# Attention: the first group's q and k buffers are filled and loaded during the norms' stage, and a third pair of score banks serves the second pass where it runs alone

## The reference

```python
x = x + _layernorm(_L0_attn_ref(_layernorm(x), ...))   # state-space block: project, scan, out_proj
h = layernorm(_layernorm(x), ln1_g, ln1_b)             # "norms' stage": this, qkv and rope
q, k, v = split(h @ Wqkv)
q, k = (rope(q), rope(k))
scores = jnp.einsum('bqhd,bkhd->bhqk', q, k) / math.sqrt(hd)
scores = jnp.where(causal, scores, -1e9)
probs = jax.nn.softmax(scores, axis=-1)
attn = jnp.einsum('bhqk,bkhd->bqhd', probs, v) @ Wproj
...                                                    # residual, norm, top-2 of 8 experts, final norm
```

## Time and profile before

| what | us |
|---|---|
| median of 3 runs | 4084.34 (4078.41 to 4086.13) |
| profiled execution: its own time | 4088.92 |
| profiled execution: span | 4087.3 |
| PE busy in the span | 3407.1 (83%) |
| DVE / ACT / POOL busy | 2777.7 / 2461.5 / 1913.2 |
| attention stage, first instruction to its last store | 2157.4 to 3394.5 |

### The profile page before, as it was taken

The page is one execution under the profiler, slowest core; times in us unless marked ns, Lnnn a source line. Parts: engine busy times, 40 slices in busy tenths (PEclk is TensorE's granted clock), DMA queues, the critical chain, the costliest instruction groups (busy, mean ns, idle before and its releaser), DMA issues. The chain is left out here.

```text
span 4087.3 us, 69747 instructions
## 1 busy us (share of the span) xinstructions
PE 3407.1 (83%) x22940; PEld 2105.2 (52%) x22940; DVE 2777.7 (68%) x4397; ACT 2461.5 (60%) x3860; POOL 1913.2 (47%) x1734
## 2 busy tenths in 40 slices
PE   7568888888888888885876999999999996499994
PEld 3246666666666666664553333333333334366663
DVE  3259999999899999995764777777777753511113
ACT  3259999999999999993220555555555563122111
POOL 1049999999899999995431000000010002512222
PEclk9779999999999999998995999999999997599997
DMA  5633333333333333335634011011011014333323
GB/s 187 187 89 97 97 99 97 95 94 96 93 96 101 96 94 94 94 94 203 221 119 124 9 20 17 9 20 20 7 20 20 7 48 132 129 81 84 86 53 93
DMA packets 162170, 349.72 MB, mean 86 GB/s; under 512 B 20963, under 2 KB 74198, under 8 KB 147344
## 3 DMA queue, kind: packets, MB, share of 16 engines
q1 hardware_dynamic: 129904, 270.96, 23.9%
q0 software_dynamic: 20624, 43.82, 4.2%
q10 hardware_dynamic: 11280, 30.41, 2.0%
HBM read 245.04 MB, written 102.59 MB: 85 GB/s over the span
## 5 line engine op out<-in xcount | busy, mean ns | idle before, releaser
L516 POOL TENSOR_TENSOR scan_hC<-scan_hh,scan_cbc 128x512 f32<-128x512 f32 x1024 | 1376.4, 1374 | 84.5 <-DVE scan_hh L728 76.8
L728 DVE TENSOR_TENSOR_SCAN scan_hh<-scan_dA,scan_state,scan_bx 128x512 f32<-128x512 f32 x1024 | 1243.5, 1263 | 140.9 <-PE scan_bx L820 63.7
L1572 PE MATMUL attend_s<-attend_kt,attend_qt 32*128 32x512 f32 (+3 forms) x2560 | 803.3, 616 | 34.4 <-DMA attend_qt<-attend_zero 27.8
L820 PE MATMUL scan_bx<-kept_ident,scan_dBxT 128*128 128x128 f32 x4096 | 668.9, 289 | 151.0 <-DVE scan_hh L728 121.9
L564 ACT ACTIVATE scan_dA<-scan_dt,scan_an 128x512 f32<-128x512 f32 x1028 | 661.4, 712 | 30.5 <-DVE scan_hh L728 30.5
L820 PEld LDWEIGHTS scan_bx<-kept_ident,scan_dBxT 128*128 128x128 f32 x4096 | 487.7, 147 | 358.8 <-DVE scan_hh L728 243.2
L831 PE MATMUL scan_acc<-kept_ident,scan_hC 128*128 128x128 f32 x4128 | 646.4, 283 | 29.6 <-POOL scan_hC L516 22.6
L1593 PE MATMUL attend_s<-attend_qt,attend_kt 32*128 32x512 f32 (+3 forms) x2560 | 643.6, 588 | 16.3 <-POOL attend_pb L1449 13.9
L569 ACT ACTIVATE scan_dBxT<-scan_dtxT,scan_bt 128x512 f32<-128x512 f32 x1028 | 655.4, 711 | 0.2
L1483 DVE TENSOR_REDUCE attend_mx<-attend_s 128x1 f32<-128x512 f32 x768 | 494.9, 686 | 203.1 <-PE attend_s L1572 202.0
L1543 ACT ACTIVATE attend_pb<-attend_s 128x1024 f32<-128x1024 f32 x384 | 390.8, 1024 | 285.9 <-PE attend_s L1593 285.9
(11 more groups left out here) (208 smaller groups left out, 3838.1 us busy)
## 6 DMA issues: line engine op xcount, KB each, us to landing
scan_xs<-scratch_xin SPq DMA_DIRECT2D x288, 256.0 KB, 6.2
scan_cbc<-scratch_crows SPq DMA_DIRECT2D x64, 1024.0 KB, 4.8
scratch_y<-scan_uu ACTq DMA_DIRECT2D x17, 1024.0 KB, 5.7
scratch_exp_in<-proj_cleared SPq DMA_DIRECT2D x8, 1044.0 KB, 8.4
experts_xt<-scratch_exp_in SPq DMA_DIRECT2D x8, 1044.0 KB, 5.2
scratch_xin<-proj_out_x SPq DMA_DIRECT2D x8, 1024.0 KB, 5.9
scratch_sz<-proj_out_z SPq DMA_DIRECT2D x8, 1024.0 KB, 6.3
mix_yf<-scratch_y SPq DMA_DIRECT2D x8, 1024.0 KB, 6.6
```

Of the source, the lines that this page charges most:

```text
L516: pool.tensor_tensor(hC[n % 2][:, m, :], h[:, m, :], rows, ALU.mult).then_inc(hc_ok, 1)
L728: dve.tensor_tensor_scan(hh[n % 2][:, m, r], dA[n % 2][:, m, r], bx[bank(l, j)][:, r], state[:, d, n, m:m + 1], ALU.mult, ALU.add).then_in ...
L820: last = pe.transpose(bx[bank(l, j)][:, t * P:(t + 1) * P], dBxT[turned_slot(l, n)][:, t, m * P:(m + 1) * P], k["ident"][:, :])
L1572: pe.matmul(s1[v % S1][:, 0:w], qt[n % SETS][rows, t * P:(t + 1) * P], kt_[n % SETS][rows, c * C:c * C + w], start=True, stop=True).then_i ...
```

## The change

It has two parts.

1. Buffers `qt` and `kt` of set 0 and their semaphore `loaded` move out of `attend` into a stage `heads` that is opened before `mix_and_qkv` and closed at the end of the program. POOL fills them as its first work in `mix_and_qkv`. After its last load there, SP waits for the fills and for the stores of four chunks, and issues group 0's q and k (8 transfers). The zero row is no longer loaded for groups 0 and 1, since q's fill is zero. In `attend` only set 1 is filled, SP starts with v, and PE waits for 8 transfers.
2. The three banks of the first pass become one tensor `s1_all`. From step 302 on (`ALONE`), when the first pass has used them last, the pairs of the second pass go round three buffers (`s1_all[:, 0:2]`, `s2_0`, `s2_1`); a pair then waits for the exponential three pairs back instead of two.

```diff
+def first_heads(s):
+    return {
+        "qt": s.sb("qt", [P, L]),
+        "kt": s.sb("kt", [P, L]),
+        "filled": s.sems("filled")[0],
+        "loaded": s.sems("loaded")[0],
+    }
+
+def load_heads(sp, qk, qt, kt, n, loaded):
+    HG = 4
+    b, g = n // (H // HG), n % (H // HG)
+    for h in range(HG):
+        rows = slice((g * HG + h) * HD, (g * HG + h + 1) * HD)
+        own = slice(32 * h, 32 * h + HD)
+        sp.dma_start(qt[own, :], qk[b, 0, rows, :]).then_inc(loaded, 16)
+        sp.dma_start(kt[own, :], qk[b, 1, rows, :]).then_inc(loaded, 16)
...
@@ mix_and_qkv, SP after its loads, and POOL at its start
+            sp.wait_ge(heads["filled"], 2)
+            for it in range(ITEMS):
+                sp.wait_ge(stored_h[it], 16 * NC)
+            load_heads(sp, qk, heads["qt"], heads["kt"], 0, heads["loaded"])
 
         @block.gpsimd
         def _(pool):
+            pool.memset(heads["kt"][:, :], 1.0).then_inc(heads["filled"], 1)
+            pool.memset(heads["qt"][:, :], 0.0).then_inc(heads["filled"], 1)
             for i in range(2):
                 pool.memset(vt[i][:, :, :, HD:], 1.0).then_inc(ones_ok, 1)
@@ attend
-        qt = [s.sb(f"qt{i}", [P, L]) for i in range(SETS)]
-        kt_ = [s.sb(f"kt{i}", [P, L]) for i in range(SETS)]
+        qt = [heads["qt"], s.sb("qt1", [P, L])]
+        kt_ = [heads["kt"], s.sb("kt1", [P, L])]
...
-        s1 = [s.ps(f"s1_{i}", [P, C]) for i in range(S1)]
+        s1_all = s.ps("s1", [P, S1, C])
+        s1 = [s1_all[:, i, :] for i in range(S1)]
...
+        ALONE = NUNIT - LEAD + 2
+
+        def pair_bank(at, pair):
+            if at < ALONE:
+                return s2[pair]
+            third = (at - ALONE) * 2 + pair
+            return s1_all[:, 0:2, :] if third % 3 == 0 else s2[third % 3 - 1]
...
-            load(0)
             for b in range(B):
                 sp.dma_start(vall[:, b * KT:(b + 1) * KT, :, :].rearrange("p t h e -> p t (h e)"),
                              vav[:, b * KT:(b + 1) * KT, :]).then_inc(loaded_v[b], 16)
...
-            for i in range(SETS):
-                pool.memset(kt_[i][:, :], 1.0).then_inc(filled, 1)
-                pool.memset(qt[i][:, :], 0.0).then_inc(filled, 1)
+            pool.memset(kt_[1][:, :], 1.0).then_inc(filled, 1)
+            pool.memset(qt[1][:, :], 0.0).then_inc(filled, 1)
             pool.memset(zero[:, :], 0.0).then_inc(filled, 1)
             pool.memset(cap_s[:, :], 3.0e38).then_inc(filled, 1)
...
-                    own, score = pb[at % PB][:, 2 * pair:2 * pair + 2, :], s2[pair]
+                    own, score = pb[at % PB][:, 2 * pair:2 * pair + 2, :], pair_bank(at, pair)
...
-                    pe.wait_ge(loaded[n % SETS], (n // SETS + 1) * HG * 3 * 16)
+                    pe.wait_ge(loaded[n % SETS], (n // SETS * 3 + 2) * HG * 16)
...
-                if at:
+                if at >= ALONE:
+                    pe.wait_ge(exp_ok, at * 2 - 2 + pair)
+                    if at == ALONE and pair == 0:
+                        pe.wait_ge(s1_read, NUNIT * HG)
+                        pe.wait_ge(m_rows, GROUPS * NC)
+                elif at:
                     pe.wait_ge(exp_ok, at * 2 - 1 + pair)
```

More of the change, by code:

```diff
@@ L1330, in qkv_layout, with attend @@
     return np.ascontiguousarray(np.concatenate([qk, w[:, :, 2].reshape(D, D)], 1))
-def attend(nc, k, qk, va, attn, load_next):
+def attend(nc, k, heads, qk, va, attn, load_next):
     KT = L // P
@@ L1374, in attend @@
         sums = [s.sb(f"sums{i}", [P, C]) for i in range(2)]
-        s1 = [s.ps(f"s1_{i}", [P, C]) for i in range(S1)]
+        s1_all = s.ps("s1", [P, S1, C])
+        s1 = [s1_all[:, i, :] for i in range(S1)]
         s2 = [s.ps(f"s2_{i}", [P, 2, C]) for i in range(2)]
         pv = s.ps("pv", [P, C])
-        pm = s1[0][0:HG * JT, 0:P]
-        loaded = s.sems(*[f"loaded{i}" for i in range(SETS)])
+        pm = s1_all[0:HG * JT, 0, 0:P]
+        ALONE = NUNIT - LEAD + 2
[4 more added lines that the diff above has]
+            return s1_all[:, 0:2, :] if third % 3 == 0 else s2[third % 3 - 1]
+        loaded = [heads["loaded"], s.sems("loaded1")[0]]
         loaded_v = s.sems(*[f"loaded_v{b}" for b in range(B)])
@@ L1393, in _ @@
         def _(sp):
-            sp.wait_ge(filled, 2 * SETS + 1)
+            sp.wait_ge(filled, 3)
             def load(n):
@@ L1398, in load @@
                     sp.wait_ge(s2_mm, (n - SETS + 1) * NSTEP * 2)
[L1399 removed]
+                load_heads(sp, qk, qt[n % SETS], kt_[n % SETS], n, loaded[n % SETS])
+                if n < SETS:
+                    return
                 for h in range(HG):
[L1401 to L1403 removed]
                     sp.dma_start(qt[n % SETS][32 * h + HD:32 * h + HD + 1, :], zero[h:h + 1, :]
@@ L1592, in scores2 @@
                     rows = slice(32 * h, 32 * h + 32)
-                    last = pe.matmul(s2[pair][:, i, o:], kt_[n % SETS][rows, kt * P:(kt + 1) * P],
+                    last = pe.matmul(pair_bank(at, pair)[:, i, o:], kt_[n % SETS][rows, kt * P:(kt + 1) * P],
                                      qt[n % SETS][rows, qc * C + o:(qc + 1) * C], start=True, stop=True)
@@ L2304, in sandwich_block, with load_next @@
                       a["dskip"])
[L2305 to L2322, removed]
-                    combine(nc, k, x3, x1t, out)
+        with Stage(nc, "heads") as around_heads:
+            heads = first_heads(around_heads)
+            mix_and_qkv(nc, k, heads, y, sz, a["u"], a["out_wT"], a["g1"], a["b1ln"], a["wqkv"], a["rope"], x1, xf, qk, va)
+            with Stage(nc, "routed") as early:
+                rt = route_inputs(nc, early)
+                def load_next(sp):
+                    load_route_weights(sp, rt, a["wproj"], a["g2"], a["b2ln"], a["wgate"], a["expert_iota"])
+                    for n in range(2):
+                        load_route_chunk(sp, rt["at"][n], rt["xt"][n], rt["loaded"][n], n, attn, xf)
+                attend(nc, k, heads, qk, va, attn, load_next)
+                with Stage(nc, "weights") as held:
+                    ew = expert_weights(nc, held)
+                    route(nc, k, rt, attn, xf, x3[0:NTOK, :], exp_in, a["token"],
+                          lambda sp, e: load_expert_weights(sp, ew, e, a["w1"], a["b1"], a["w2"], a["b2"]))
+                    with Stage(nc, "last") as last:
+                        x1t = [last.sb(f"x1t{n}", [P, JT, D]) for n in range(B * NC)]
+                        run_experts(nc, k, ew, exp_in, a["w1"], a["b1"], a["w2"], a["b2"], x3, x1, x1t,
+                                    last.sems("loaded_x1")[0])
+                        combine(nc, k, x3, x1t, out)
```

4 lines of the change are left out of this document (2 added, 2 removed).

## The result

| | us | runs |
|---|---|---|
| before | 4084.20 median (4078.41 to 4086.13) | 4 |
| after | 4061.34 median (4058.54 to 4066.37) | 4 |
| ratio | 0.9948, 95% interval 0.9930 to 0.9965 | |

The account below looks back on a forecast made before the run. No engine bounds the whole program, its stages following each other through barriers. Handover 14.3 plus second pass 4.5 less closing block 0.6 made 18.2 us off 4084.34, so 4066.1 us; 8-in-10 range 4057 to 4075.

Parts of the forecast that it names:

- the 14.3 us: Handover to the attention: PE's first matmul comes 14.3 us earlier, waiting for `caps_ok` alone instead of fills and transfers.
- The extra fills in the norms' stage: Start of the norms' stage: two fills cost POOL 3.6 us, covered by waiting for first loads; price 0.
- The closing block: End of the program: closing `heads` adds one more block, +0.6 us, bounds 0.3 and 1.5.
- the row of a step that had no wait: Second pass alone: the 2.32 us step, scores 1.39 us, taken as the length of every whole step.
- PE works through: Second pass alone: with three buffers both waits are met and PE bounds each whole step at 2.32 us.
- ACT idle 0.38: Second pass alone: ACT, needing 1.94 us for two exponentials, idles 0.38 us in each 2.32 us step.
- The gain in the 12 whole steps: Last query chunk: 12 whole steps fall from 2.64 to 2.32 us each, 3.8 us off.
- The last four steps: End of the second pass: ACT bounds these steps, and its pauses of 0.52 and 0.18 us go, 0.7 us.
- both times for scores that waited for a buffer: Last four steps: the reason given for ACT's pauses of 0.52 and 0.18 us, so a third buffer removes 0.7 us.
- −4.5: Step 302 to the last evacuation: all of part 2, 3.8 us from whole steps plus 0.7 from the last four.
- the sum: Whole program: 14.3 + 4.5 − 0.6 = 18.2 us off, unchanged by the skill's clock rule.
- its first rival: First pass alone: the clock rises within it after PE's shorter pause, giving 4054 us; chance 0.04.

Follow-up runs that it names:

- e2: The kernel before with only the third pair of banks and its waits added, nothing of the handover; 4079.24 us, ratio 0.9982.
- e6: The changed kernel with ACT taking the exponential of only half the columns in the whole steps from 302 on; one run, 4056.24 us.
- e7: The changed kernel with the next step's first pair of scores ahead of the values on PE in the last 18 steps; 4056.63 us, ratio 0.9935.
- e1: The changed kernel with only the handover, the third pair buffer never used; 4071.65 us, ratio 0.9962.
- e10: The changed kernel with `cap_s` made first and only two pair buffers to the end; 4066.86 us, ratio 0.9961.
- e3: The changed kernel with POOL making `cap_s` before its other fills and SP loading v without waiting for fills; 4060.76 us, ratio 0.9939.
- e8: The changed kernel with group 0's eight transfers back at the head of `attend`, without a wait for a fill; one run, 4063.2 us.
- e5: The changed kernel with four extra full-array matmuls in each of the 20 units the first pass works alone; 4101.3 us, ratio 1.0038.

## Why the prediction was right

**Part 1 was right term by term.** Of the 14.3 us, 14.36 came, in a chain that ended where it was said to end, at POOL's `cap_s`. The extra fills in the norms' stage came out of POOL's idle 10.90 us, and the stage grew by 0.20 us of 277. A price of some tenths up to 2 us is not excluded: this stage scatters between 275.7 and 279.2 us in the ten profiles with `heads`, and has 276.8 and 274.6 in the two without. PE started 0.05 us after `cap_s` was ready, where 0.1 had been assumed. The closing block cost 0.70 against 0.6; kernels without the stage `heads` (before, e2) have 42.74, those with it 43.42 to 43.65.

**Part 2 was right in what frees the step, and off in both sizes.** That the two pair buffers were the limit held: with a third, none of the ten steps has scores of 2.03 us any more. The whole steps were forecast at 2.32 us, "the row of a step that had no wait". That row had one: its scores took 1.39 us in the earlier trace rows, and in e6, where ACT has half the work, they take 1.14. One row of before's tail had shown less than 1.39:

```profile
3350.11 1.22 PE L1593 MATMUL attend_s<-attend_qt,attend_kt 32*128 32x512 f32 x8
```

The mis-sized term is this step: PE's own pace is 2.08, the measured mean is 2.185, since two steps hold four exponentials and a pause, 4.01 + 0.36 us. So "PE works through" and "ACT idle 0.38" a step did not come: PE waits for ACT in every second step, and ACT is idle 0.18 a step. The gain in the 12 whole steps was 5.05 us (0.49 in the stretch up to the step at 3340.16, 4.56 in the ten after it), not 3.8. The last four steps gave 11.49 − 11.43 = 0.06 us, not 0.7. The step that failed there is "both times for scores that waited for a buffer": for the pause of 0.53 us, the scores of step 318 (3367.76) stand on PE behind the values of step 316 (3366.76), which wait for POOL's mask, and a third buffer doesn't change that; e7 changed the order and the pause went. The pause of 0.18 us shows no such releaser at all ("issue" in the earlier trace rows). That −5.11 came so near to −4.5 is in part luck: the two errors, 1.2 us too little and 0.6 too much, nearly cancel.

**What was in no sum.** The routing row became 3.29 us shorter, and nothing of the change is in it. It has two pieces. In the routing stage and up to the experts' first matmul on the weights 1.49 us went, 1.0 of them in the first chunk, where PE's first sixteen records take 6.62 us in before and 5.65 in after. The stage's first matmuls run at 0.50 until the clock rises. Windows of before, whose routing starts at 3401.73:

```profile
3410.00:3412.00 2.00, 2.00 (x6) 1.62 (x5) 0.00 (x0) 0.00 (x0) 0.00 (x0) 0.50 0.53 132
3412.00:3414.00 2.00, 2.00 (x7) 1.58 (x6) 0.00 (x0) 0.00 (x0) 0.00 (x0) 0.58 0.49 172
```

and of after, whose routing starts at 3381.78:

```profile
3390.00:3392.00 2.00, 2.00 (x7) 1.54 (x6) 0.00 (x0) 0.00 (x0) 0.00 (x0) 0.56 0.31 72
3392.00:3394.00 2.00, 1.44 (x7) 0.93 (x5) 0.52 (x1) 0.00 (x0) 0.00 (x0) 1.00 0.88 243
```

1.00 is reached some 12 us after the stage's start in before and 10 us in after. The other 1.80 us lie behind the stage, in the experts' first matmuls. Before, then after:

```profile
3577.31 5.47 PE L2186 MATMUL experts_ph<-experts_xT,weights_w1t 128*128 128x512 f32 x8 [0.88 <-DVE experts_xT L2113]
```

```profile
3555.87 3.67 PE L2224 MATMUL experts_ph<-experts_xT,weights_w1t 128*128 128x512 f32 x8 [0.87 <-DVE experts_xT L2151]
```

The same eight records take 5.47 us in before, where the first four last 1.06 to 1.19 us each, and 3.67 in after, where all but the first last 0.59; 1.06 and 0.59 are the lengths of the 512-wide matmul before and after the clock has risen in the earlier trace rows. From the first of them to ACT's table load before has 3.84 us, after 2.04. The two pieces behave differently in the twelve profiles. The routing stage up to its closing block takes 165.0 to 165.6 us in the three kernels without the third buffer (before, e1, e10) and 163.1 to 164.2 in the nine with it. The experts' piece takes 3.8 us in those three, but 3.7 in e3 and e8 too, which have the third buffer, and 2.04 in the other seven. So what goes with the third buffer, in single executions, is about 1.5 us; that it causes them is not shown, nor is why the last steps of the attention should set the moment at which the clock rises some 10 us into the next stage.

The second pass beside the first gave −3.30 us in the two profiled executions. Here too the granted clock differs. The times between evacuations agree within 0.02 us almost everywhere; only those around a group's start take one of a few values. Before, windows that hold a start:

```profile
2545.00:2569.00 24.00, 22.15 (x141) 8.44 (x137) 12.87 (x34) 10.39 (x23) 3.67 (x6) 0.54 0.24 39
...
2840.00:2856.00 16.00, 12.84 (x133) 5.22 (x129) 11.49 (x32) 9.52 (x21) 3.67 (x6) 1.00 0.29 51
```

A group's start is the time from one group's last evacuation to the next group's first (18.93 and 13.62 us in these two). The seven starts sum to 112.8 us in before, 108.3 in after, and between 99.6 and 112.0 in the others, whatever their parts. That is how scatter of single executions looks and not the change, though before was profiled once only; that it makes up most of what runs of one kernel differ by (7.7 us in before, 7.8 in after) is likely and not shown.

**The clock.** In all runs the first pass alone stays at the 1.2 GHz level. The Trainium skill, page "TensorE: Matmul & The Clock Gate", section "Part 1: The HAM clock gate (the "warmup" mystery)", has the default as throttled and sustained activity as what releases it. PE's 72 busy us of 75 here, and e5's 20.00 of 20 with full-array matmuls among them, do not release it; the measurement decides. So the forecast was right to leave the sum alone, and its first rival to get 0.04.

## What to carry to other kernels

When an engine waits at a stage's head, list the whole chain ahead of its first instruction and ask of each link whether it needs the stage at all: fills and loads of a fixed buffer can go into the previous stage's waiting time, and of those that remain, the one that the critical engine wants goes first (5.94 us became 0.71 by order alone). A third buffer is worth at most the difference between the step that waits and the larger of the two engines' own times (here 2.64 − 2.08 a step, of which 0.46 came); take that own time from the shortest instance of each piece (scores 1.22 us in before's tail, 1.14 in e6), not from the shortest whole step. When a pause stays with more buffers, as the 0.53 us here, look at the order in the queue. Before a difference between two profiles is put down to a change, find the rows in which it lies, and see whether they move in other kernels that have the change.

## What was not expected of the hardware

- The granted clock stayed at 0.50 over 75 us of PE busy 96% of the time, and in e5 over 117 us, 20.00 of 20 us busy in one window.
- When it rises after a pause differs by about 2 us between kernels that run the same instructions from there on, and the experts' first eight matmul records took 5.47 us in one profile and 3.67 in another.
- A group's start takes one of a few lengths between 13.6 and 18.9 us, within one execution and between kernels with the same instructions there.
